# Geometric attention in rectangular rows, one running maximum over signed keys, and one transpose of the output

## What is computed

```
q, k, v = heads of xn @ Wq.T, xn @ Wk.T, xn @ Wv.T;  q, k rotated (rope)
out     = softmax(causal(q k^T / sqrt(d))) v
qp = q[..., :3] . head_dirs;   kp = k[..., :3] . head_dirs
geo     = causal(qp[..., :, None] * kp[..., None, :])
geo_out = softmax(geo) v
out     = out + head_scales * (geo_out - out)
x       = x + out @ Wo.T
```

## Time and profile before

| | us |
|---|---|
| median of 3 runs | 2190.05 |
| lowest and highest | 2188.83, 2192.83 |
| span of the profiled execution, first to last instruction | 2242.6 |
| attention phase within that span | about 100 to 660 |

### The profile page before, as it was taken

How to read it: one execution, slowest core, us unless ns; L and a number is a source line. 1 busy time by engine, 2 the same in 40 slices (tenths; PEclk the granted TensorE clock), 3 DMA queues, 4 the chain that set the end, 5 groups by cost and what they waited for, 6 DMA issues and landing times. The chain is left out here.

```text
span 2242.6 us, 44681 instructions
## 1 busy us (share of the span) xinstructions
PE 1743.5 (78%) x13783; PEld 1370.5 (61%) x13783; DVE 1650.1 (74%) x4953; ACT 1349.8 (60%) x3266; POOL 1185.3 (53%) x1272
## 2 busy tenths in 40 slices
PE   5688999899976656949994777777777651999994
PEld 5577777777753442426662555555566541999993
DVE  7599999999966982438986999999755432555554
ACT  4577777777744993228772788888444331556551
POOL 3277777877740004842314788888724455444440
PEclk8699999999986756969997999999865555999997
DMA  3000000000013112341200000000220111222217
GB/s 112 12 2 2 2 2 2 2 2 2 2 52 121 39 39 56 48 113 57 66 10 1 1 1 1 1 1 1 78 106 30 34 38 57 70 66 64 66 51 230
DMA packets 103368, 92.05 MB, mean 41 GB/s; under 512 B 11696, under 2 KB 93744, under 8 KB 102432
## 3 DMA queue, kind: packets, MB, share of 16 engines
q1 hardware_dynamic: 80128, 62.77, 9.1%
q0 software_dynamic: 14560, 22.24, 3.8%
q10 hardware_dynamic: 8448, 4.20, 0.6%
HBM read 46.26 MB, written 42.91 MB: 40 GB/s over the span
## 5 line engine op out<-in xcount | busy, mean ns | idle before, releaser
L2263 POOL TENSOR_TENSOR delta_A<-delta_A,delta_sW 128x256 f32<-128x256 f32 x256 | 193.4, 755 | 78.9 <-ACT delta_sW L2110 52.8
L2033 PE MATMUL delta_u<-delta_m,tables_sb 128*128 128x256 f32 x512 | 166.3, 407 | 82.1 <-DVE delta_m L2183 82.1
L2883 POOL DMA_INDIRECT choice_rows<-ffn_y,ffn_xg x135 | 128.7, 953 | 170.8 <-DVE ffn_y L2990 165.6
L644 ACT ACTIVATE attn_p_att<-attn_score,attn_mx 128x224 f32<-128x224 f32 (+7 forms) x512 | 146.6, 394 | 102.3 <-DVE attn_mx L735 102.3
L630 ACT ACTIVATE attn_p_geo<-attn_kp_wide,attn_geo_cols 128x32 f32<-128x32 f32 (+6 forms) x448 | 179.0, 482 | 2.5
L573 PE MATMUL attn_score<-attn_k,attn_q_diag 128*128 128x64 f32 (+5 forms) x1024 | 177.8, 317 | 0.0
L2110 ACT ACTIVATE delta_sW<-delta_W,tables_sb 128x256 f32<-128x256 f32 x256 | 126.6, 506 | 79.6 <-DVE delta_W L2205 75.8
L2033 PEld LDWEIGHTS delta_u<-delta_m,tables_sb 128*128 128x128 f32 x512 | 87.2, 190 | 132.4 <-DVE delta_m L2183 125.7
L2029 PE MATMUL delta_u<-delta_v_own,tables_sb 128*128 128x256 f32 x512 | 153.6, 382 | 9.6 <-DVE xnT L2170 9.6
L2840 POOL DMA_INDIRECT rows<-mix_rows,mix_slot x128 | 124.6, 973 | 56.8 <-issue 52.5
L573 PEld LDWEIGHTS attn_score<-attn_k,attn_q_diag 128*128 128x128 f32 x1024 | 149.5, 193 | 7.3
(11 more groups left out here) (401 smaller groups left out, 5044.8 us busy)
## 6 DMA issues: line engine op xcount, KB each, us to landing
ffn_xg<-rows SPq DMA_DIRECT2D x135, 66.0 KB
acc<-route_zero SPq DMA_DIRECT2D x10, 832.0 KB
comb_rows<-choice_rows SPq DMA_DIRECT2D x32, 256.0 KB
rows<-route_rows SPq DMA_DIRECT2D x8, 640.0 KB, 3.4
load_rows<-in_x SPq DMA_DIRECT2D x16, 256.0 KB, 4.9
bT<-acc SPq DMA_DIRECT2D x16, 256.0 KB, 4.1
qT<-acc SPq DMA_DIRECT2D x16, 256.0 KB, 4.9
x_kept<-xT SPq DMA_DIRECT2D x16, 256.0 KB, 2.1
```

Source lines behind the costliest of these rows:

```text
L644: last = nc.scalar.activation(p_att[:, gr, PAIR_OFF[n]:PAIR_OFF[n] + SLOT * (n + 1)], score[at][:, c:c + SLOT * (n + 1)], ACT.Exp, bias=mx ...
L2033: nc.tensor.matmul(corrections(h, pp % 2), g.t("same_head"), m1[:, h].rearrange("p t d b -> p (t d b)"), start=False, stop=True).then_inc( ...
L2263: nc.gpsimd.tensor_tensor(A[:, t % 8], A[:, (t - 1) % 8], sW[:, t % RING], ALU.add).then_inc(k.A, 1)
L2883: nc.gpsimd.indirect_dma_start(g.choice_rows, bass.IndirectOffsetOnAxis(xg[:, n % RING, D:D + 1].bitcast(U32), 0), y[:, n % RING, :], None ...
```

## The change

1. **Signed key rows, one scan.** `dirs` gets one more matrix. In the 32 partitions of a head, slot gr holds qp of group gr in the query rows (nothing in the key rows). Slots 2+2gr and 3+2gr now hold -qp and +qp in the query rows and kp and -kp in the key rows (the signs are set on the device once). One running maximum over the key rows, which starts at 1.0 in slots 0 and 1 and at -3e38 elsewhere, gives 1, max(kp) and -min(kp). GpSimd multiplies it by the query rows once: qp, -qp max(kp), -qp min(kp). This tile is transposed (256 wide), and the minimum of the two bounds is taken afterwards, on 16 elements per partition. `run_min`, `less_qp` and their instructions are gone.
2. **Rectangular rows.** `p_geo` holds a row of 256 keys per query block, cleared once; own blocks are written into it by a strided exponential. `turn_geo` turns two query blocks at once in 4 instructions, over 40 blocks of 32, instead of 8 instructions over 36.
3. **One output tile.** The two PSUM tiles `O` become one of two banks, transposed by one instruction.

```diff
+    f["scan_start"] = np.where(slot < GROUPS, 1.0, -3e38)[:, None]
...
-        p_geo = s.sb("p_geo", [128, GROUPS, EARLY_OFF[KB]])
-        p_own = s.sb("p_own", [128, GROUPS, KB, SLOT])
         PITCH = T + SLOT
+        p_geo = s.sb("p_geo", [128, GROUPS, KB * PITCH])
...
-        O = [s.ps(f"out{pair}") for pair in range(PAIRS)]
+        O = s.ps("out", (128, PAIRS, GROUPS * T))
...
             def front_qk(b):
-                pe.wait_ge(k.less_qp, b)
+                pe.wait_ge(k.rows_copied, b)
...
-                nc.tensor.matmul(q_rows_ps[:, T:2 * T], dirs[:, 0, :], kk[:, par, :], start=True, stop=True).then_inc(k.rows_made, 1)
+                nc.tensor.matmul(q_rows_ps[:, T:2 * T], dirs[:, 1, :], kk[:, par, :], start=True, stop=True).then_inc(k.rows_made, 1)
...
                 for n in range(1, KB):
-                    nc.scalar.activation(p_geo[:, gr, EARLY_OFF[n]:EARLY_OFF[n + 1]],
+                    nc.scalar.activation(p_geo[:, gr, n * T:n * T + SLOT * n],
...
-                nc.scalar.activation(p_own[:, gr], geo_own[:, par, gr], ACT.Exp).then_inc(by_group[gr].geo_exp, 1)
+                nc.scalar.activation(p_geo[:, gr, :].rearrange("p (n i) -> p n i", i=PITCH)[:, :, 0:SLOT], geo_own[:, par, gr], ACT.Exp).then_inc(by_group[gr].geo_exp, 1)
...
-                act.wait_ge(k.ga_made, b)
-                act.wait_ge(k.gb_made, b)
-                nc.scalar.activation(less_qp[:, :], q_rows_ps[:, 0:T], ACT.Copy, scale=-1.0).then_inc(k.less_qp, 1)
...
+            nc.vector.memset(p_geo[:, :, :], 0.0).then_inc(k.cleared, 1)
+            dve.wait_ge(k.cleared, 4)
...
+            for kind in range(2):
...
+                nc.vector.tensor_scalar(minus, minus, -1.0, None, ALU.mult).then_inc(k.signed, 1)
...
-                nc.vector.tensor_tensor_scan(run_max[:, :], kp, kp, -3e38, ALU.max, ALU.max).then_inc(k.ran_max, 1)
-                nc.vector.tensor_tensor_scan(run_min[:, :], kp, kp, 3e38, ALU.min, ALU.min).then_inc(k.ran_min, 1)
+                nc.vector.tensor_tensor_scan(run_max[:, :], kp, kp, g.t("scan_start"), ALU.max, ALU.max).then_inc(k.ran_max, 1)
...
-                nc.vector.tensor_tensor(geo_rows[:, 1, :], run_max[:, :], run_min[:, :], ALU.min).then_inc(k.less_max, 1)
...
-                nc.vector.transpose(geo_cols[:, par].rearrange("p s n i -> p (s n i)"),
-                                    geo_rows[:, :, :].rearrange("p s t -> p (s t)")).then_inc(k.geo_cols, 1)
+                nc.vector.transpose(geo_cols[:, par].rearrange("p n i -> p (n i)"), run_max[:, :]).then_inc(k.cols_turned, 1)
+                dve.wait_ge(k.cols_turned, b + 1)
+                low = geo_cols[:, par, :, BOUND:BOUND + 2 * GROUPS].rearrange("p n (g s) -> p n g s", s=2)
+                nc.vector.tensor_tensor(low[:, :, :, 0], low[:, :, :, 0], low[:, :, :, 1], ALU.min).then_inc(k.geo_cols, 1)
...
-                for n in range(1, KB):
-                    nc.vector.transpose(by_key(1, gr)[:, 0:n, SLOT * n:SLOT * n + SLOT],
-                                        p_geo[:, gr, EARLY_OFF[n]:EARLY_OFF[n + 1]].rearrange("p (j i) -> p j i", i=SLOT))
-                nc.vector.transpose(turned[:, 1, gr, :].rearrange("p (n i) -> p n i", i=PITCH)[:, :, 0:SLOT], p_own[:, gr])\
-                    .then_inc(by_group[gr].geo_turned, 1)
+                for n in range(0, KB, 2):
+                    last = nc.vector.transpose(by_key(1, gr)[:, 0:n + 2, SLOT * n:SLOT * n + 2 * SLOT]
+                                               .rearrange("p j (n i) -> p n j i", n=2),
+                                               p_geo[:, gr, n * T:(n + 2) * T].rearrange("p (n j i) -> p n j i", n=2, i=SLOT)
+                                               [:, :, 0:n + 2, :])
+                last.then_inc(by_group[gr].geo_turned, 1)
...
-                nc.vector.transpose(oT[:, pair].rearrange("p n i -> p (n i)"), O[pair][:, :]).then_inc(k.out_turned, 1)
+                nc.vector.transpose(oT[:, :].rearrange("p o n i -> p (o n i)"), O[:, :, :].rearrange("p o t -> p (o t)"))\
+                    .then_inc(k.out_turned, 1)
...
-                nc.gpsimd.tensor_tensor(run_max[:, :], run_max[:, :], less_qp[:, :], ALU.mult).then_inc(k.ga_made, 1)
-                pool.wait_ge(k.ran_min, b + 1)
-                nc.gpsimd.tensor_tensor(run_min[:, :], run_min[:, :], less_qp[:, :], ALU.mult).then_inc(k.gb_made, 1)
+                nc.gpsimd.tensor_tensor(run_max[:, :], run_max[:, :], geo_rows[:, 0, :], ALU.mult).then_inc(k.bounds_made, 1)
```

More of the change, by code:

```diff
@@ L464 @@
 PAIRS, HALF = PER // 2, 2 * SLOT
+BOUND = GROUPS
 PAIR_OFF = [SLOT * (2 * (n // 2) * (n // 2 + 1) + n % 2 * (2 * (n // 2) + 2)) for n in range(KB + 1)]
-EARLY_OFF = [SLOT * n * (n - 1) // 2 for n in range(KB + 1)]
 def attention_phase(nc, dram, g):
@@ L475, in attention_phase @@
         wo = s.sb("wo", [128, PAIRS, 128])
-        dirs = s.sb("dirs", [128, 1 + GROUPS, 128])
+        dirs = s.sb("dirs", [128, 2 + GROUPS, 128])
         hs = s.sb("hs", [128, PAIRS * GROUPS])
@@ L486, in attention_phase @@
         geo_rows = s.sb("geo_rows", [128, 2, T])
-        less_qp = s.sb("less_qp", [128, T])
         run_max = s.sb("run_max", [128, T])
-        run_min = s.sb("run_min", [128, T])
-        geo_cols = s.sb("geo_cols", [128, 2, 2, KB, SLOT])
+        geo_cols = s.sb("geo_cols", [128, 2, KB, SLOT])
         kp_wide = s.sb("kp_wide", [128, 2, GROUPS, KB, SLOT])
@@ L505, in attention_phase @@
         q_rows_ps, k_wide_ps, v_out_ps = (s.ps(name) for name in ("q_rows", "k_wide", "v_out"))
-        O = [s.ps(f"out{pair}") for pair in range(PAIRS)]
-        k = s.sems("w_in cleared ones share_ready q_made k_made v_made rows_made kp_made tq tk q_ready k_ready v_turned"
-                   " rows_copied less_qp kp_copied ran_max ran_min ga_made gb_made less_max geo_cols geo_own"
+        O = s.ps("out", (128, PAIRS, GROUPS * T))
+        k = s.sems("w_in cleared signed ones share_ready q_made k_made v_made rows_made kp_made tq tk q_ready k_ready v_turned"
+                   " rows_copied kp_copied ran_max bounds_made cols_turned geo_cols geo_own"
                    " recip coef combined out_turned summed out_made gated x_done")
@@ L586, in weigh @@
                         for kind in range(2):
-                            last = nc.tensor.matmul(O[pair][HALF * kind:HALF * kind + HALF, gr * T + SLOT * n:gr * T + T],
+                            last = nc.tensor.matmul(O[HALF * kind:HALF * kind + HALF, pair, gr * T + SLOT * n:gr * T + T],
                                                     v_diag[rows, gr, n], turned[rows, kind, gr, n * T + SLOT * n:(n + 1) * T],
@@ L803, in _ @@
                     front_cols(b + 1, 1 - par)
-                for pair in range(PAIRS):
-                    turn_out(b, pair)
+                turn_out(b)
             coefs(B - 1)
@@ L867, in geo @@
                 shape = [128, GROUPS, KB, SLOT]
-                by_query = [geo_cols[:, par, n, :, 0:GROUPS].rearrange("p n g -> p g n")[:, :, :, None].to_broadcast(shape)
-                            for n in range(2)]
+                rate = geo_cols[:, par, :, 0:GROUPS].rearrange("p n g -> p g n")[:, :, :, None].to_broadcast(shape)
+                bound = geo_cols[:, par, :, BOUND:BOUND + 2 * GROUPS].rearrange("p n (g s) -> p g n s", s=2)[:, :, :, 0:1]\
+                    .to_broadcast(shape)
                 pool.wait_ge(k.geo_cols, b + 1)
                 pool.wait_ge(k.kp_copied, b + 1)
-                nc.gpsimd.tensor_tensor(geo_own[:, par], kp_wide[:, par], by_query[0], ALU.mult).then_inc(k.geo_own, 1)
+                nc.gpsimd.tensor_tensor(geo_own[:, par], kp_wide[:, par], rate, ALU.mult).then_inc(k.geo_own, 1)
                 pool.wait_ge(k.geo_own, 3 * b + 1)
-                nc.gpsimd.tensor_tensor(geo_own[:, par], geo_own[:, par], by_query[1], ALU.add).then_inc(k.geo_own, 1)
+                nc.gpsimd.tensor_tensor(geo_own[:, par], geo_own[:, par], bound, ALU.add).then_inc(k.geo_own, 1)
                 pool.wait_ge(k.geo_own, 3 * b + 2)
```

44 lines of the change are left out of this document (25 added, 19 removed).

## The result

| | before | after |
|---|---|---|
| median us | 2190.83 (4 runs) | 2166.27 (4 runs) |
| lowest and highest | 2188.83, 2192.83 | 2164.46, 2167.53 |
| ratio with 95% interval | | 0.9887 [0.9875, 0.9899] |
| span of the profiled execution | 2242.6 | 2165.0 |
| attention phase in it, first clear to last instruction | 100.1 to 662.2 | 98.6 to 632.6 |

The change gains 24.6 us; 42 were forecast, and 2166.3 lies above the range. The profiled execution of before had lost some 50 us in the mix phase, long after attention (1612 to 1891 us, 279 us; after it the same phase takes 229), which is where its distance from the median came from. The two attention phases can be compared: 562.1 and 534.0 us, 28.1 less. Outside attention the profiled executions of all other runs take between 1623 and 1634 us, though no edit aims there.

The account below looks back on a forecast made before the run. VectorE bounded attention at 16.79 us a batch; afterwards a three-engine round would, at about 15.45. Periods -44.5, first batch -1.3, clearing +3.9 net -42 us off 2190.05: forecast 2148, range of 8 in 10 2138 to 2162.

Parts of the forecast that it names:

- VectorE's terms: Attention, per batch: running minimum -0.58 us, minimum and transpose -0.85, geometric transposes -0.20, output -0.03 to -0.07.
- Rival B: Contention with GpSimd moves onto the new small minimum, or strided transposes gain nothing: period 15.7 us, 2157; chance 0.12.
- VectorE falls from 16.79 to about 15.1 us: VectorE's work per attention batch after all its savings, with the product in coefs at up to 0.74 us.
- The round of three engines: GpSimd, TensorE, VectorE over two attention batches: 5.48 + 10.23 + 0.06 + 15.1, sum 30.9 us, 15.43 a period, the longest bound.
- 31 periods: First to last start of geo_cols: 523.5 us before, 479.0 at 15.45 a period, -44.5 us.
- rival C: Product in coefs loses its contention, 0.19 us for 0.74: round and TensorE both 15.2 us, 2141; chance 0.09.
- The start: First attention batch: -1.3 us for VectorE's wait and longer minimum and transpose, +3.9 us for clearing p_geo.
- D: TensorE's clock keeps falling in attention, about 1.2 us a fall: eight falls 2158, every second batch 2167; chance 0.13.
- E: Slower: TensorE's clock falls in every attention batch at the pause for q, period 17.2 us, 2202; chance 0.03.
- TensorE alone needs 15.2 us: TensorE's own work per attention batch: 16.79 us less its pause of 1.57, and its busy 15.21; level with VectorE.
- The sum against the median: Net -42 us in attention, taken unchanged off the median of 2190.05 us, giving 2148.
- the rule weighed ahead: Small minimum forecast at 0.19 us, since GpSimd's addition should end before it; by the contention rule alone it could cost the long value.

Follow-up runs that it names:

- e8: Kernel before with only the rectangular rows turned two query blocks at once, the single output transpose, and a small p_geo clear: 2187.03 us, 0.9982.
- e1: Changed kernel with the new one-column table scan_start placed behind all other tables: 2147.86 us, 0.9805 to the kernel before.
- e3: Changed kernel with GpSimd's q and k additions ahead of combine, and coefs behind the transpose of the values: 2130.77 us, 0.9724 to the kernel before.
- e6: e1 with only the 256 p_geo columns cleared that are read and never written: 2145.65 us, 0.9791 to the kernel before.
- e7: e6 with the two moved steps of e3: 2129.84 us, 0.9714 to the kernel before.
- e11: Changed kernel with 15 unused table columns behind scan_start, so mask_own lies 16 columns further than before: 2152.06 us, one run.
- e12: e7 with GpSimd's spread_values also ahead of combine: 2129.92 us, 0.9725 to the kernel before.

## Why the prediction was wrong

The direction, the bound and the list of removed work were right; the size was not. Step by step:

- **VectorE's terms.** Right. The small minimum, at 341.03, takes 0.19 us as forecast, with GpSimd idle beside it; the 256-wide transpose 0.43 for 0.39; the output 1.25 in one; the geometric transposes cost as the dense ones (e8). The scan takes 0.70 for 0.64. Rival B, contention on the small minimum, did not come.
- **"VectorE falls from 16.79 to about 15.1 us": the step that failed.** It carried the product in coefs over at its old length, 0.74 at most. The product takes 1.16 us in one batch and 0.41 in the next, so VectorE needs 15.64 us from 342.12 to the end of geo_cols at 357.76, and 14.90 in the following batch.
- **The round of three engines.** The mechanism was right: a round of two batches, which the alternation shows, and VectorE waits 0.9 and 0.27 us ahead of the output's transpose. Its sum was too small. There are two such rounds, one batch apart. The one without a wait, which binds, takes VectorE's long batch. Forecast 5.48 + 10.23 + 0.06 + 15.1 = 30.87. Measured from geo_cols at 357.76: 5.67 to TensorE's geometric matmul at 363.43, 10.22 to the end of the second weigh, 0.17 to turn_out at 373.82, and 15.64 of VectorE: 31.70, two periods of 15.85. Of the 0.83 us more, 0.54 are VectorE's (0.42 of them the product at 1.16 for 0.74), 0.19 the longer third step, 0.11 the release of turn_out. The other round has slack: TensorE waits 0.51 us ahead of a weigh for transposes that the long product made late. In e1 the same terms are 5.48, 10.22, 0.17 and 14.68, together 30.55.
- **31 periods.** 479.0 forecast, 492.7 measured: 13.7 of the missing 17.4 us. With the table column mended (e1) they are 476.3, or 15.37 a period, between the forecast's 15.43 and rival C's 15.2.
- **Rival C was asked the wrong way.** It said that the product may lose its contention, a gain, and priced the loss nowhere. The upper bound of 0.74 us was the longest value in the trace, but the trace held the rule for a longer one: the product ends with GpSimd's instruction, so its bound is the longest GpSimd instruction that it can meet, 1.10 us or more, plus its own 0.05. The reading that 0.19 belongs to the stage's end was short too: eight of its nine cases lie in the middle, and show that the length follows the phase between the two engines.
- **The start.** The clear was +3.9 as forecast, and VectorE's idle 0.91 us ahead of it was not in the sum. From the first clear to the first geo_cols it was 16.3 us before and is 19.5 now: +3.2 for a forecast of +2.6.
- **The table column.** Nothing in the prediction asked what a shifted table does. Its 0.19 us per step would be small; through the held product it decided 16 us of the attention phase.
- **The clock, D and E.** The granted clock of TensorE was 1.00 in all steady stretches after the change: the pause for q shrank from 1.57 to 0.1 and 0.6 in turn, and no fall followed it. That TensorE alone needs 15.2 us was too high: full, it has periods of 14.84 (e3). Its busy time of 15.21 held 0.4 us that is no need of its own; the ends of its products are modelled in a trace, and what the 0.4 us are was not looked into.
- **The sum against the median.** The phase fell by 28.1 us, the median by 24.6. The missing 3.5 us stay open. They are within what the rest of the program differs by from execution to execution (1623 to 1634 us), and the ratio's interval is 2.6 us wide to each side.

On the rule weighed ahead: the Trainium skill (SBUF — State Buffer, Who interferes with whom) has a VectorE instruction with two SBUF inputs contend with a GpSimd instruction that reads SBUF. The traces agree. In the 13 executions that have the product, all 300 products that start with more than 0.14 us of GpSimd's instruction left end 0.045 to 0.053 us after it. By the same section of the Trainium skill the order of issue decides which of the two blocks, and the traces have the other side as well: GpSimd's first bound product, begun 0.21 us into VectorE's second scan, took 0.97 us before, and takes 0.73 now that no such scan runs beside it. The prediction applied the rule to the new instruction, where it did not bite, and not to the old one whose phase the change moved.

## What to carry to other kernels

In these traces the short VectorE product with two SBUF inputs costs what is left of the GpSimd instruction that it meets. So bound such an instruction by the longest one that it can meet, for the old instructions too, and ask anew for each change that moves the phase between the two engines. When a change lifts one engine's load to near that of the others, write out the round through all engines with its waits, and look for the one that has none; here two moves in the written order (e3) were worth 29 us of the attention phase and 36 of the median, more than the change itself. And put new small tables behind the old ones: a shift of 4 bytes lengthened an instruction that nobody had touched.

## What the runs showed of the hardware that was not expected

- The 128x32 product on VectorE took anything from 0.19 to 1.17 us in the changed kernel. It ended 0.04 to 0.05 us after the GpSimd instruction that was running at its start. It took 0.19 us when it started between two such instructions, or with 0.14 us or less of one left (e1).
- A longer instruction is held in the same way: the 128x256 minimum of the kernel before takes 0.41 us by itself. When it starts with 0.40 us of GpSimd's addition to x left, it takes 0.69 and ends 0.28 after it. Both end later than GpSimd's instruction by their own length less 0.13 to 0.14 us.
- GpSimd's 128x512 addition of a broadcast 32-column table took 1.10 us with the table at its old place or 64 bytes further, 1.29 us at 4 bytes further and 1.27 at 8.
- One period in each of e1, e3, e6, e7, e11 and e12, the 25th, is 1.0 to 1.4 us longer than its neighbours without a fall of the clock. Most of this is the held product again. In the 24th batch the output's transpose starts 0.52 us after the last weigh for 0.17 in the others, and the product then meets the third step. In e3:

```profile
479.44 1.29 POOL L876 TENSOR_TENSOR attn_geo_own<-attn_geo_own,tables_sb 128x512 f32<-128x512 f32 x1
479.53 1.25 DVE L774 TENSOR_TENSOR attn_coef<-attn_coef,attn_share 128x32 f32<-128x32 f32 x1
```

The product takes 1.25 us for 0.23, and with the late start's 0.35 this is the whole 1.36 by which that period is longer. Why the transpose starts late there stays open.
